# A fused cross-attention and expert layer: the turns of the softmax over 16 heads written in another order, with more of its tile copies on VectorE

## The reference, cut to what matters

```python
# x 8x224x512, ctx 8x750x512, mask 8x1x224x750; 16 heads of 32
Q = rope(layernorm(x) @ W_q.T); K = rope(ctx @ W_k.T); V = ctx @ W_v.T
scores = Q @ K.T / sqrt(32);  scores = where(mask == 0, -inf, scores)
x = x + tanh(g_xattn) * (softmax(scores) @ V) @ W_o.T
affinity = softmax(layernorm(x) @ gate_w.T)          # 8 experts
gating, idx = top_k(affinity, 56)                    # 56 rows of each batch for each expert
x = x + tanh(g_ffn) * sum over experts(gating * (silu(x_in @ w_gate.T) * (x_in @ w_up.T)) @ w_down.T)
```

## Time and profile before

| | us |
|---|---|
| median of 3 runs | 1975.56 |
| lowest, highest | 1974.62, 1976.33 |
| the profiled execution's own time | 1977.62 |
| its span | 1975.7 |
| PE busy (share of the span) | 1774.2 (90%) |
| PE weight loads busy | 1555.4 (79%) |
| VectorE busy | 1011.5 (51%) |
| ScalarE busy | 867.6 (44%) |
| GpSimd busy | 204.7 (10%) |

### The profile page before, as it was taken

One profiled execution on the slowest core, in us unless ns is written; L12 is line 12 of the kernel. 1 busy time (PEld: TensorE's weight loads), 2 busy tenths in 40 slices (PEclk: granted clock), 3 DMA queues, 4 the chain that ended last, 5 costly groups with the idle time before them and its releaser, 6 DMA issues. The chain is left out here.

```text
span 1975.7 us, 28464 instructions
## 1 busy us (share of the span) xinstructions
PE 1774.2 (90%) x10502; PEld 1555.4 (79%) x10502; DVE 1011.5 (51%) x1737; ACT 867.6 (44%) x1547; POOL 204.7 (10%) x286
## 2 busy tenths in 40 slices
PE   7999966888887888888469999999999999999995
PEld 6989865666666676666269999999999999999995
DVE  6666644656656566475335354443535445354441
ACT  3232312857666667577034343333434334343340
POOL 0000002202202112020010020200202001020101
PEclk9999986999999999999679999999999999999998
DMA  5545447545555455442043353432534334353431
GB/s 220 194 181 187 174 154 185 122 103 130 141 134 136 102 136 144 99 122 75 24 162 108 106 144 114 127 125 96 145 115 133 112 103 142 106 142 114 117 107 19
DMA packets 76187, 251.87 MB, mean 127 GB/s; under 512 B 10784, under 2 KB 10784, under 8 KB 74816
## 3 DMA queue, kind: packets, MB, share of 16 engines
q1 hardware_dynamic: 64096, 216.55, 36.4%
q0 software_dynamic: 12000, 34.12, 7.3%
HBM read 188.01 MB, written 51.61 MB: 121 GB/s over the span
## 5 line engine op out<-in xcount | busy, mean ns | idle before, releaser
L1352 PE MATMUL gu_ps<-xs_hi,ws_hi 128*128 128x448 f32 x1024 | 372.3, 364 | 3.0 <-DVE xs_lo L1287 3.0
L1354 PE MATMUL gu_ps<-xs_hi,ws_lo 128*128 128x448 f32 x1024 | 372.4, 364 | 0.0
L1353 PE MATMUL gu_ps<-xs_lo,ws_hi 128*128 128x448 f32 x1024 | 371.0, 362 | 0.0
L741 DVE CUSTOM_DVE_ANT_0 sm<-m_ps,mq 112x752 f32<-112x752 f32 x256 | 235.5, 937 | 205.7 <-PE m_ps L1012 203.6
L1282 DVE TENSOR_TENSOR ws_lo<-w_raw,ws_hi 128x1024 fp32r<-128x1024 f32 x192 | 235.4, 1226 | 188.6 <-ACT ws_hi L1232 186.9
L1232 ACT ACTIVATE ws_hi<-w_raw 128x1024 fp32r<-128x1024 f32 x192 | 201.8, 1051 | 163.8 <-PE y_ps L1371 146.6
L1028 PEld LDWEIGHTS t_ps<-cst,sm 112*125 112x125 f32 x1536 | 216.9, 196 | 60.9 <-issue 44.9
L645 ACT ACTIVATE e_t<-t_ps 125x448 f32<-125x448 f32 x320 | 171.3, 541 | 202.1 <-PE t_ps L1028 202.1
L1028 PE MATMUL t_ps<-cst,sm 112*125 112x112 f32 x1536 | 247.3, 287 | 11.0 <-issue 7.2
L638 ACT ACTIVATE sm<-sm,least 112x752 f32<-112x752 f32 x256 | 234.3, 916 | 7.7 <-DVE least L741 7.7
L1352 PEld LDWEIGHTS gu_ps<-xs_hi,ws_hi 128*128 128x128 f32 x1024 | 192.7, 188 | 15.4 <-issue 3.3
(11 more groups left out here) (125 smaller groups left out, 2368.1 us busy)
## 6 DMA issues: line engine op xcount, KB each, us to landing
w_raw<-wstream SPq DMA_DIRECT2D x192, 512.0 KB, 3.5
ks<-k_split SPq DMA_DIRECT2D x192, 188.0 KB, 6.1
k_split<-k_split SPq DMA_DIRECT2D x32, 752.0 KB, 3.5
v_rows<-v_out SPq DMA_DIRECT2D x16, 750.0 KB
vs<-v_rows SPq DMA_DIRECT2D x16, 750.0 KB
c_raw<-ctxT SPq DMA_DIRECT2D x7, 1500.0 KB, 12.8
qs<-q_hi POOLq DMA_DIRECT2D x64, 112.0 KB, 2.9
mq_raw<-maskq SPq DMA_DIRECT2D x8, 656.2 KB, 11.1
```

The costliest lines, as they stand in the source:

```text
L741: nc.vector.tensor_tensor_reduce(sm[:, h % SR, qc].rearrange("p (a n) -> p a n", a=2), m_ps[qc][0:QP, :, 0:KN], mq[:, qc].rearrange("p (a ...
L1352: nc.tensor.matmul(o, w_hi[s][:, w], xs_hi[:, c], start=(c == 0), stop=False)
L1353: nc.tensor.matmul(o, w_hi[s][:, w], xs_lo[:, c], start=False, stop=False)
L1354: mm = nc.tensor.matmul(o, w_lo[s][:, w], xs_hi[:, c], start=False, stop=(c == DC - 1))
```

## The change

In PE's turn `values` moves to directly behind tile 0, both `scores` go behind tile 1; `project_q` and `project_out` are cut in halves and put into other turns. In VectorE's turn `normalise` and the tile copies go ahead of `mask_scores`; a table `DVE_TILES` gives VectorE 16 tiles of a batch in place of 8. ScalarE makes the exponentials two heads ahead (`XLEAD` = 2) in place of one. The sum of Q, its low part and the addition of the flag to the output stay on VectorE; POOL gets nothing new to compute. The other pieces of work get other turns, on POOL and SP too. The condition of a tile copy on the last quad's values stands once per engine and quad (`opens`), and `values` wait for the last copy of each of the two engines (`quad_emptied`). The gate's last step (`affinity`) comes a batch later, and the waits for the two stores move from the batch's end to the instructions that need them.

```diff
-DVE_TILE = 1
-DVE_SLOTS = (0, 1, 2, 4, 7, 9, 11, 13)
+XLEAD = 2
+DVE_TILES = {0: (0, 1, 2), 1: (1,), 2: (1,), 6: (1, 2), 7: (0, 1), 8: (0,), 10: (2,), 11: (1,), 12: (1,), 13: (0,), 14: (0,), 15: (1,)}
...
@@ SP, body
+                        if t == 0 and not last:
+                            load_x(b + 2)
+                        if t == 0 and not first:
+                            load_res(b - 1)
...
-                        if t == 4 and not last:
-                            load_x(b + 2)
-                        if t == 4 and not first:
-                            load_res(b - 1)
@@ POOL, body
+                            if t in (3, 4):
+                                sines(b + 1, t - 3)
+                            if t == 4:
+                                root(b + 2, 0, 2 if first else 2 * b + 1)
+                            if t == 7:
+                                stack_q(b + 1, 0)
+                                stack_q(b + 1, 1)
...
+                            if t == 8:
+                                root(b - 1, 1, 2 * b + 1 if last else 2 * b + 2)
+                            if t == 9:
                                 store_rows(b - 1)
-                            if t == 13:
                                 store_out(b - 1)
@@ ACT, body
-                            if t + 1 < H:
-                                exp(b, t + 1, qc)
+                            if t + XLEAD < H:
+                                exp(b, t + XLEAD, qc)
...
-                            if pc == 0 and t % HG == 1:
...
+                        if t % HG == 0:
+                            if t >= HG:
+                                copy_parts(b, t // HG - 1)
@@ DVE, body
+                        if t % HG == 0:
+                            if t >= 2 * HG:
+                                normalise(b, t // HG - 2)
+                            elif not first:
+                                normalise(b - 1, t // HG + 2)
+                        for pc in range(KC // 2):
+                            if on_dve(t, pc):
+                                empty(b, t, pc)
                         if not last and t + MLEAD == H:
                             mask_queries(b + 1)
                         for qc in range(QC):
...
-                            if qc == 0 and on_dve(t, DVE_TILE):
-                                empty(b, t, DVE_TILE)
-                        if t % HG == 0:
...
-                        if t % HG == HG - 1:
+                        if t % HG == 2:
                             invert(b, t // HG)
...
-                            if t == 14:
-                                next_moments(b + 2)
-                            if t == 15:
+                            if t == 12:
                                 next_norm(b + 2)
...
-                                affinity(b - 1, 1 - j)
-
-                                dve.wait_ge(out_stored, 16 * b)
-                                dve.wait_ge(rows_stored, 16 * b)
@@ PE, body
                         turn_rows(b, t, 0)
-                        next_scores(0)
-                        turn_rows(b, t, 1)
-                        next_scores(1)
                         if t % HG:
                             last_values()
+                        turn_rows(b, t, 1)
+                        next_scores(0)
+                        next_scores(1)
                         turn_rows(b, t, 2)
                         if t % HG == 0:
                             last_parts()
...
+                            if t in (2, 3):
+                                project_q(b + 1, 0, t - 2)
+                            if t == 4:
+                                project_q(b + 1, 1, 0)
+                                project_q(b + 1, 1, 1)
                         if not first:
+                            if t == 5:
+                                project_out(b - 1, 0, 0, last)
+                                project_out(b - 1, 0, 1, last)
                             if t in (6, 7):
-                                project_out(b - 1, t - 6, last)
-                            if t in (11, 12):
-                                turn_x2(b - 1, t - 11)
+                                project_out(b - 1, 1, t - 6, last)
+                            if t in (10, 12):
+                                turn_x2(b - 1, t // 2 - 5)
```

160 lines of the change are left out of this document (83 added, 77 removed).

## The result

The changed kernel takes 1875.53 us (median of 4 runs, 1873.91 to 1875.96) beside 1975.35 us for the kernel before in the same comparison: a ratio of 0.9493, 95% interval 0.9476 to 0.9509. The profiled execution took 1875.96 us, its span is 101.8 us shorter than that of before.

What follows compares the result with a forecast made beforehand. PE was taken as the bound: 61.7 us of work plus 8.0 of remaining waits gives 70 a middle body. Savings of 57 (six middle), 3 (first) and 8 (last) sum to 68, so 1908 us, range 1884 to 1938.

Steps and rivals of the forecast that it cites:

- The full-speed body: Time a middle body would take if PE never waited, summed from its pieces of work: 61.7 us, unchanged by the change.
- Turn 0: VectorE starts late and copies tile 0 after PE wants its buffer: 1.0 us a middle body left.
- Turn 8: The residual and low_q of turn 7 stand ahead on VectorE: 0.9 us a middle body left.
- Turns 10 to 14: Tight turns on ScalarE and VectorE, where a late copy holds the tile after next: 1.3 us a middle body left.
- Copy of the sums: Values wait while copy_parts follows ScalarE's last copy: 0.6 us in each of three quads, 1.8 a middle body left.
- Two tiles without values between: In four turns the first tile has only the last tile's copy time: 0.3 to 0.4 us each, 1.4 a body.
- Clock behind the logits: PE's reduced clock behind the gate's logits, kept although the fall after the long stall should go: 1.6 us a middle body.
- B: Rival: PE comes nearer its bound, with 5 us a body left, 21 us more gained, 1887 us; chance 14%.
- A: Rival: half the stalls stay as late copies add up, 13 us a body left, 1943 us; chance 18%.
- C: Rival: VectorE's copies hold up its masks, 88 us a body, 57 us slower, 2033 us; chance 4%.
- D: Rival: PE at half clock through turns 8 to 15, 84 us a body, 32 us slower, 2008 us; chance 2%.
- E: Rival: nothing changes, as new waits match the old, 1975 us; chance 2%.

Runs made afterwards that it cites:

- a_pool_q_f9_x2: Changed kernel with Q's sum and low part on POOL, VectorE's flags in turn 9, x2_out in turn 14, output store in turn 15; 1867.95 us.
- a_8tiles: Changed kernel with the earlier tile table, 8 copies a body on VectorE and 40 on ScalarE; 1882.85 us, ratio 0.9535.
- b_chain: Kernel before with normalise first, exponentials two heads ahead, and VectorE's chains of turns 14 and 15 moved to other turns; 1930.6 us.
- b_norm_first: Kernel before with only VectorE's normalise moved to the head of its turn, ahead of the masks; 1959.25 us, ratio 0.9914.
- a_last0: Changed kernel with normalise put back behind both masks in turn 0 alone; 1910.78 us, ratio 0.9668.
- a_last12: Changed kernel with normalise put back behind both masks in turn 12 alone; 1896.41 us, ratio 0.9599.
- a_pool_q: Changed kernel with the sum of Q and its low part on POOL in place of VectorE, same turns; 1891.06 us, ratio 0.9577.
- a_pool_q_f9: Changed kernel with the sum of Q and its low part on POOL and VectorE's flags in turn 9, not 6; 1869.71 us, ratio 0.9463.

## Why the prediction was right, and where it was not

The forecast was 1908 us with a range from 1884 to 1938; 1875.53 lies below it. The place of the loss and the direction were right, the sum of what would stay was twice too large.

**Where the loss stood: right.** The six middle bodies gave 84 of 102 us, and of the causes named `cx` has gone, the copy of the sums nearly (1.0 + 0.9 us in five bodies) and the clock is at 1.00. The clean turn is unchanged (3.06 us), and so are the experts. That no engine but PE would bind was right too.

**The full-speed body, 61.7 us: right within what the trace can tell.** A body now takes 65.67 us with 3.7 of named waits and gaps, 4.0 above the sum of its matmuls. The other reckoning, by weight loads, would have put it at 51.6 us and the kernel at 1780; PE's weight loads are busy for 50.3 of the 65.7 us now, and of all the kernels tried the fastest has a median of 1867.95 us.

**What stays, 8.0 us a body: wrong, it is 4.0.** This is the step that failed; the terms one by one, as the prediction put them:
- Turn 0, 1.0 us: 0.65 + 0.20 of waits, 1.05 to 1.25 with their gaps. Right.
- Turn 8, 0.9: 0.76, with its gap 0.96, behind `low_q` and the residual. Right.
- Turns 10 to 14, 1.3: 0.47 + 0.19 in turn 12, with gaps about 1.0. Right, and by a_pool_q_f9_x2 `x2_out` is what made these two.
- Copy of the sums, 1.8: 0.25 in one turn, with its gap 0.45. Mis-sized: I let `copy_parts` follow ScalarE's last copy in each quad, though the new table takes tiles from ScalarE in exactly these turns, 0, 8 and 12. a_8tiles has the wait I had reckoned with: 12.5 us in 320, against 1.9.
- Two tiles without values between, 1.4: no row shows a wait of this kind outside the places above. The gap I put in was not there.
- Clock behind the logits, 1.6: nothing. This was the largest error in kind. I took the fall at 622 us for a thing that comes behind the logits in each body and without a long wait ahead. Neither holds in the trace of before. Two waits stood ahead of it, in turns 12 and 13:

```profile
616.69 0.41 PE L1036 MATMUL o_ps<-cst,spread 112*128 112x112 f32 x2 [1.78 <-DVE cx L764]
...
619.75 0.96 PE L1055 MATMUL o_ps<-e_t,vs 125*32 125x224 f32 x16 [0.71 <-issue]
```

And of the six middle bodies, which all have the same logits, the clock fell behind them in two only (at 622 and 783 us). In a third it fell at the wait of turn 12 already (698 us), in the other three not at all, though their two waits were much the same (1.46 to 1.48 and 0.71 to 0.72 us). Read from body 3 and taken six times, the term was three times too large even for the kernel before. In the changed kernel the two waits are gone (0.47 and 0.19 us stand in turn 12), and the clock stays behind the logits of all six middle bodies. So the logits alone do not make it fall; why it fell in some of the bodies with such waits and not in others stays open.

The last three terms are 4.3 us too much, the first three came out as reckoned, and some 0.3 us lies in no wait that the trace names: 4.0 a body. By the bodies' own times that is 84.2 us against 57; 2 us of the difference is the rounding of 69.7 up to 70.

**First body 3: 3.2. Last body 8: 12.6. The end 0: 2.9.** The last body's clock rose from 0.95 to 1.00. The prediction let 9.5 of its 17.5 us stay; before it had waits of 7.8 us for `cx` in turns 0, 4, 8 and 12 and 5.4 of others, 13.2 in all, and now has 3.7 in all. In the end the chain was not left as it is: its first wait for `cx` is 1.08 us in place of 2.05, and the fall of the clock behind it lasts 3.4 us in place of 10.2. Less 1.1 us for the experts the sum is 102 against 68.

**The rivals.** B (5 us left, 1887) was nearest and still 11 us too high. It got 14% because the forecast took each unknown wait at its full size. A fell. C fell: with sixteen copies a body ahead of the masks PE waits 0.9 us for masks in 320 us. D did not come about in the change; something near it, two falls of the clock in each body with waits of at most 1.4 us, is what b_chain shows. E fell.

**The signs I looked for.** The bodies came out at 65.5, not 68 to 72; VectorE is 4.0 us busier a body and ScalarE 3.4 less; no clock near 0.5 in the middle bodies; PE's waits spread over the tile copies, none over 1 us at the same turn of each middle body.

**What the parts are worth.** They are not additive. Undone one at a time they cost 87, 12, 12 and 7 us; done on the kernel before, `normalise` gave 16, the exponentials 6, both 29, with the chains 45, with PE's order 54. While other waits stand in the body, removing one can shift PE onto the next, as b_norm_first shows, and the mean clock stayed between 0.91 and 0.97 in all these runs on the kernel before; in the changed kernel it is 1.00, and putting `normalise` back takes it to 0.92. The parts tried make 54 of the 100 us; the other 45 come with the table and the new turns of the remaining pieces together.

## What to carry to other kernels

Cost what remains from the full-speed sum up, term by term, and ask of each term whether the change also moves what makes it; a leftover guessed from the old trace at its full size was twice what came. In a kernel bound by PE, price a wait at the wait and the clock behind it, but read the clock from every repetition and not from one: the same wait brought a fall in some bodies and none in others. Undo a part in the new kernel before you judge it by adding it to the old one: `normalise` was worth 16 us in the one and 87 in the other.

## What the runs showed of the hardware

- With a wait of 2.74 us of PE in each body (a_last0) the clock fell to half in all seven bodies, for 3.4 to 10.2 us, in part before the wait was over; with one of 1.53 us (a_last12) in four bodies of seven, for 3.4 us each. Waits of 0.72 and 0.60 us followed by the logits went with a fall in all five middle bodies looked at (b_chain), waits of 1.15 and 1.03 us without logits with none in six (before), and waits up to 0.76 us with none over six bodies (the changed kernel).
- A VectorE operation on two elements a partition took 2.20 us, in place of 0.17, while GpSimd ran a subtraction of 128x896 values on two SBUF inputs (a_pool_q, seven bodies of eight). In a_pool_q_f9, where the same subtraction runs on GpSimd among VectorE's masks and tile copies, which read PSUM, none of them was held: the 256 masks took 0.943 us at most, the 128 copies 0.626.
- The 128x896 subtraction takes 2.08 us on GpSimd and 1.09 us on VectorE. Where GpSimd has time, it is still the better place here for the sum and the low part of Q, by 6 us, once the flags stand in another turn.
